# Scoring twice in the second attention of a macaron layer: by queries for the maximum, by keys for the exponential

## Chip, cores and metric

The kernel runs on one core of a Trainium2 chip. The metric is the device time in microseconds (us), the median of several executions. Three executions of the kernel before took 834.92, 836.00 and 836.39 us; the median is 836.0.

## What is computed

Two layers run one after the other on an input of 4 x 256 tokens with 256 features. Each is a macaron layer: half a feed-forward network, self-attention, half a feed-forward network, each behind a layer norm.

```python
x = x + 0.5 * ffn0(layernorm(x))          # silu(gate) * up
x = x + attn0(layernorm(x))               # 16 heads of 128, 4 key/value heads, window
x = x + 0.5 * ffn0(layernorm(x))
x = x + 0.5 * moe(layernorm(x))           # 8 experts, top 2, and a shared expert
x = x + attn1(layernorm(x))               # 16 heads of 16, causal
x = x + 0.5 * moe(layernorm(x))
```

The change lies in `attn1`, the second attention:

```python
qkv = einsum('bld,ed->ble', x, W_qkv); q, k, v = split(qkv, 3)     # to 4 x 16 heads x 256 x 16
q, k = rope(q), rope(k)
att = einsum('bhqd,bhkd->bhqk', q, k) * 16 ** -0.5
att = where(causal, att, -inf)
y = einsum('bhqk,bhkd->bhqd', softmax(att), v)
out = einsum('bld,ed->ble', y, W_o)
```

## The kernel before

The 1,024 tokens are 8 tiles of 128. A half, `hf`, is a pair of the four sequences, so 4 tiles. The kernel is one program in which every engine has its own list of instructions, written by hand; semaphores order them (`wait_ge`, `then_inc`; `after(engine, sem, n)` is a wait that is left out where it would be trivial). The six stages are told by their turn number: turn 4 is the layer norm and turning ahead of the second attention, turn 5 turns the attention's result for the output projection, turn 6 is ahead of the last feed-forward network, whose routing (`route_logits`, `prefix`, `routing_slots`, `routing_weights`, `scatter`, all with 6 and a half) is threaded through the attention's second half.

**The second attention** runs half 0 (about 581 to 630 us), then projections, rotations and turnings of half 1's queries and keys, then half 1 (about 657 to 704 us), then the output. `half(hf)` goes through 16 heads; a step, `step1(hf, p, q)`, is head g = 4p + q of the half, for both sequences of it, and every engine has its own `step1`. For each sequence the score block is causal: two query tiles of 128, the first against 128 keys, the second against 256, so 384 columns a sequence, 768 a step, in two banks of PSUM.

A head goes through these operations:

- TensorE, `scores_of`: four score matmuls with queries as weights (L1804) and four that add the mask (L1808); scores of even heads lie in banks 2hf and 2hf+1, those of odd heads in 4 and 5.
- VectorE: two maximum reductions, negated, into `MB1` (L1369).
- TensorE, the shift: four matmuls with the identity `IDB` as weights and the maximum, broadcast along the columns, as the moving operand add minus the maximum to the scores in PSUM (L1843).
- ScalarE: one exponential over the 768 columns into `PR1`, f32 (L896).
- TensorE: six f32 transposes, one for each block of 128 x 128, into banks 6 and 7 (L1821), two heads behind.
- ScalarE copies the turned probabilities as f16 (L891, `PT1[., 0]`), VectorE subtracts that from PSUM for the f16 remainder (L1375, `PT1[., 1]`).
- TensorE, the values: 18 matmuls of 17 columns (16 features and the sum of the row), three heads behind (L1504, in the helper `product`).
- VectorE: reciprocal of the sum and multiplication (L1385, L1390).

In TensorE's list, step g holds the transposes of head g-2, the values of head g-3, the shift of head g, and the scores of head g+1. `lagged(p, q, n, P1)` says whether a head n behind exists.

**Other work in the halves.** VectorE does the sums and statistics of turn 4 for half 1 (`turn_stats(4, 1, .)`) after steps 0 and 1 of half 0 and its norms (`turn_norm`, L1048) after steps 5 and 7; TensorE's `turn(4, 1)` comes near that half's end. In half 1 TensorE does `prefix(6, 0)` after step 0 (L1542, L1547) and VectorE the slots after step 0 (`routing_slots`, L1099 to L1113) and the weights after step 4 (`routing_weights`, L1138 to L1145). GpSimd's list has, for the halves, only turn 4's reciprocal roots (L522, L525) and, in half 1, `scatter(6, 0)`: eight indirect DMAs (L561) that write the tokens to the rows of their experts. Outside the halves GpSimd works in the rotations (L631, L639, L641).

`ARENA` is a region of SBUF that the stages share; the second attention keeps `PR1` (two buffers of 768 f32) and `PT1` (two buffers of two parts of 768 f16) there.

Of the kernel before, what the change touches and what calls it, by code (L numbers as in the profile page):

```python
# [88 lines left out]
def macaron(nc, x_in, wa_in, wb_in, wc_in, wd_in, wg_in, rope0_in, rope1_in, mask_in, idf_in,  # L89
# [3 lines left out]
    with ctx:  # L93
# [45 lines left out]
        ARENA = sb("ARENA", [P, 3584], F32)  # L139
# [7 lines left out]
        PT1 = ARENA[:, 1536:3072].bitcast(F16).rearrange("p (a s n) -> p a s n", a=2, s=2)  # L147
# [106 lines left out]
        exp1_done, pt1_done, pt1_hi, pt1_lo = (sem(n) for n in ("exp1_done", "pt1_done", "pt1_hi", "pt1_lo"))  # L254
# [184 lines left out]
        def pt1_part(a, s, i):  # L439

            return PT1[:, a, s, i * BLK1 * P:(i + 1) * BLK1 * P]

# [66 lines left out]
        def _(pool):  # L509
# [133 lines left out]

            turn(0, 0)
# [25 lines left out]
            turn(4, 1)  # L670
# [5 lines left out]
            scatter(6, 0)  # L676
# [7 lines left out]
        def _(act):  # L684
# [200 lines left out]
            def step1(hf, p, q):  # L885
                g = NG1 * hf + 4 * p + q
                if lagged(p, q, 2, P1):
                    after(act, pv1_done, g - 3)
                    for i in range(2):
                        act.wait_ge(pt1_done, 2 * g - 3 + i)  # L890
                        sc.activation(pt1_part(q % 2, 0, i), PS[:, 6 + i, 0:BLK1 * P], ACT.Copy).then_inc(pt1_hi, 1)  # L891
                if lagged(p, q, 0, P1):

                    act.wait_ge(shifted1, g + 1)
                    bank = 4 if q % 2 else 2 * hf
                    sc.activation(PR1[:, q % 2, :].rearrange("p (b n) -> p b n", b=2),  # L896
                                  PS[:, bank:bank + 2, 0:384], ACT.Exp, bias=LNSP[:, :],
                                  scale=SC1 / SQ ** 2).then_inc(exp1_done, 1)

            def attention1():  # L900
                def half(hf):
                    for q in range(4):
                        step1(hf, 0, q)
                    with act.Fori(1, P1) as p:
# [5 lines left out]
                    step1(hf, P1, 1)  # L910
# [62 lines left out]
        def _(dve):  # L973
# [388 lines left out]
            def step1(hf, p, q):  # L1362
                g = NG1 * hf + 4 * p + q
                a = q % 2
                if lagged(p, q, 0, P1):
                    dve.wait_ge(scores1, g + 1)
                    bank = 4 if a else 2 * hf
# [3 lines left out]
                item, turned_item = lagged(p, q, 3, P1), lagged(p, q, 2, P1)  # L1371
# [6 lines left out]
                if turned_item:  # L1378
                    low(0)
                if item:  # L1380
# [5 lines left out]
                if turned_item:  # L1386
                    low(1)
                if item:
# [4 lines left out]
            def attention1():  # L1393
                def half(hf):
# [11 lines left out]
                    with dve.Fori(2, P1) as p:  # L1406
                        for q in range(4):
                            step1(hf, p, q)
                    for q in range(3):
# [88 lines left out]
        def _(pe):  # L1498
# [299 lines left out]

            def scores_of(hf, p, q):
                bank = 4 if q % 2 else 2 * hf  # L1800
                after(pe, exp1_done, NG1 * hf + 4 * p + q - 1)
                for i in range(2):
                    for qt, c0 in ((0, 0), (1, P)):
                        te.matmul(PS[:, bank + i, c0:c0 + (qt + 1) * P],  # L1804
# [3 lines left out]
                        ins = te.matmul(PS[:, bank + i, 2 * c0:2 * c0 + P], IDB[:, :], MASK[:, :], start=False,  # L1808
                                        stop=False, skip_group_check=True)
                ins.then_inc(scores1, 1)  # L1810

            def step1(hf, p, q):
                g = NG1 * hf + 4 * p + q
                a = q % 2
                bank = 4 if a else 2 * hf
# [34 lines left out]
                elif q == 3 and lagged(p + 1, 0, 0, P1):  # L1850
                    scores_of(hf, p + 1, 0)
# [198 lines left out]
```

## Time and profile before

| | |
|---|---|
| median of three executions | 836.0 us (834.92 to 836.39) |
| span of the profiled execution | 835.5 us |
| TensorE matmul busy | 718.3 us, 86% of the span |
| TensorE weight load busy | 483.5 us, 58% |
| VectorE busy | 628.1 us, 75% |
| ScalarE busy | 458.0 us, 55% |
| GpSimd busy | 402.9 us, 48% |
| second attention, half 0 | about 581 to 630 us |
| second attention, half 1 | about 657 to 704 us |

The profiled execution has no time of its own beside its span, which lies 0.5 us under the median of the others. In the profile PE is TensorE's matmuls and PEld its weight loads (which overlap), DVE is VectorE, ACT ScalarE, POOL GpSimd, SP the engine that issues plain DMAs. PEclk is the granted TensorE clock, 1.00 for 2.4 GHz and 0.50 for 1.2 GHz. In a timeline a row is one instruction, or a run of like ones (x4), with its start in the span, its length, its engine, its line and what it writes and reads; brackets hold the idle time ahead of it and who ended it. Shares over the whole span say little about one stage; what the change is worth is read in the two halves.

### The profile page before, as it was taken

The page shows a single profiled execution, that of the slowest core. Times are in us where ns is not written, and L with a number is a line of the kernel's source. Part 1 is how long each engine was busy: PE and PEld are TensorE (multiplying, and loading weights), DVE is VectorE, ACT ScalarE, POOL GpSimd, SP SyncE. Part 2 cuts the span into 40 slices and gives each one's busy share as a digit, 9 for nine tenths or more (in the row PEclk, how much of TensorE's full clock was granted, in tenths as well). Part 3 has the DMA queues.
Part 4 walks back from the last instruction along what each step waited for, and adds up shares of the span by engine and source line. Part 5 has one row for each costly group of instructions (what it writes and reads, how often), then busy time and mean ns, then how long its engine had stood idle before and what let it go on. Part 6 is the DMA issues. An engine that isn't in the chain of part 4 may idle for free. (4 is left out here: it accounts for less than half of the span.)

```text
span 835.5 us, 17560 instructions
## 1 busy us (share of the span) xinstructions
PE 718.3 (86%) x5515; PEld 483.5 (58%) x5515; DVE 628.1 (75%) x1436; ACT 458.0 (55%) x1033; POOL 402.9 (48%) x412
## 2 busy tenths in 40 slices
PE   7898959999979999989898699855897598988985
PEld 3454437777636777755455466433785487545652
DVE  5989878778787778698987577543898596775646
ACT  3444568887757788646423266325574475324541
POOL 4545766767666676358636277424005320331440
PEclk8999989999989999999999799976799598998997
DMA  9999994000000000030001243300000010013324
GB/s 371 328 303 182 241 216 2 0 0 0 1 1 1 0 0 0 1 120 1 1 14 51 77 116 109 133 1 1 1 2 1 18 35 2 2 61 88 115 84 151
DMA packets 64945, 59.07 MB, mean 71 GB/s; under 512 B 29106, under 2 KB 59186, under 8 KB 64370
## 3 DMA queue, kind: packets, MB, share of 16 engines
q1 hardware_dynamic: 60706, 47.85, 23.5%
q0 software_dynamic: 3744, 10.26, 3.5%
q8 instruction: 36, 0.59, 0.3%
q14 instruction: 27, 0.22, 0.1%
q10 hardware_dynamic: 432, 0.15, 0.1%
HBM read 27.92 MB, written 30.33 MB: 70 GB/s over the span
## 5 line engine op out<-in xcount | busy, mean ns | idle before, releaser
L1504 PE MATMUL PS<-XT,WA 128*128 128x512 f16 x432 | 101.2, 382 | 0.0
L611 POOL TENSOR_TENSOR ARENA<-ARENA,ST 128x512 f32<-128x512 f32 x64 | 66.6, 1040 | 65.5 <-DVE ST L1284 65.5
L729 ACT ACTIVATE ARENA<-T 128x512 f16<-128x512 f32 (+1 forms) x56 | 35.2, 628 | 109.2 <-DVE T L1162 101.7
L1504 PE MATMUL PS<-WA,ARENA 128*128 128x256 f16 (+2 forms) x960 | 68.4, 213 | 12.7 <-DVE ARENA L1171 11.7
L1504 PEld LDWEIGHTS PS<-WA,ARENA 128*128 128x128 f16 x960 | 56.6, 97 | 29.0 <-DVE ARENA L1171 17.6
L570 POOL DMA_INDIRECT yt_rows<-WA,DIX x46 | 45.4, 987 | 55.0 <-ACT WA L861 41.0
L1504 PEld LDWEIGHTS PS<-XT,WA 128*128 128x128 f16 (+1 forms) x432 | 42.6, 99 | 44.9 <-issue 2.1
L1264 DVE TENSOR_REDUCE ST<-PS 128x2 f32<-128x512 f32 x64 | 44.0, 687 | 27.7 <-PE PS L1504 26.7
L1504 PE MATMUL PS<-KVR,ARENA 128*128 (+1 forms) x384 | 58.2, 280 | 7.5 <-DVE ARENA L1256 4.6
L1504 PE MATMUL PS<-XT,WC 128*128 128x512 f16 x264 | 62.3, 387 | 2.4 <-DVE T L1155 1.4
L762 ACT ACTIVATE ARENA<-PS,ST 128x256 f32<-128x256 f32 x128 | 59.3, 470 | 7.0 <-DVE ST L1267 6.8
L599 POOL TENSOR_TENSOR T<-T 128x512 f32<-128x512 f32 x40 | 52.6, 1315 | 8.1 <-DVE T L1250 2.6
L594 POOL TENSOR_TENSOR T<-T,ROPE 128x512 f32<-128x512 f32 x40 | 50.9, 1271 | 10.4 <-ACT T L743 10.3
L1171 DVE TENSOR_TENSOR ARENA<-T,ARENA 128x512 f16<-128x512 f32 (+1 forms) x48 | 43.0, 896 | 16.1 <-ACT ARENA L729 15.6
L1504 PE MATMUL PS<-ARENA,KVR 128*128 128x256 f16 x384 | 52.4, 272 | 2.5 <-DVE ARENA L1287 2.5
L1504 PE MATMUL PS<-XT,WB 128*128 128x512 f16 x192 | 48.5, 391 | 6.2 <-DVE T L1250 4.8
L1504 PE MATMUL PS<-WB,ARENA 128*128 (+1 forms) x384 | 52.4, 273 | 0.3 <-DVE ARENA L1287 0.3
L1155 DVE SCALAR_TENSOR_TENSOR T<-T,PS 128x512 f32<-128x512 f32 (+1 forms) x56 | 38.1, 680 | 18.8 <-ACT T L721 18.4
L721 ACT ACTIVATE T<-PS 128x512 f32<-128x512 f32 (+1 forms) x56 | 33.1, 592 | 33.9 <-PE PS L1504 33.7
L1504 PE MATMUL PS<-WE,WA 128*128 x276 | 50.1, 318 | 0.0
L1504 PE MATMUL PS<-WC,ARENA 128*128 128x256 f16 (+1 forms) x288 | 41.0, 299 | 8.9 <-DVE ARENA L1171 8.8
L1504 PEld LDWEIGHTS PS<-KVR,ARENA 128*128 128x128 f16 x384 | 33.0, 100 | 26.5 <-issue 7.4
(184 smaller groups left out, 1799.5 us busy)
## 6 DMA issues: line engine op xcount, KB each, us to landing
xs_rows<-ROUT SPq DMA_DIRECT2D x2, 9252.0 KB, 45.9
WA<-xs_rows SPq DMA_DIRECT2D x46, 129.0 KB
WB<-wb_dram SPq DMA_DIRECT2D x1, 4096.0 KB, 21.6
WC<-wc_dram SPq DMA_DIRECT2D x1, 2304.0 KB, 27.3
WA<-wa_dram SPq DMA_DIRECT2D x4, 512.0 KB, 7.3
WA<-wa_dram SPq DMA_DIRECT2D x1, 2048.0 KB, 12.9
WA<-yt_rows SPq DMA_DIRECT2D x4, 512.0 KB, 4.1
WB<-yt_rows SPq DMA_DIRECT2D x4, 512.0 KB, 6.0
```

Of the source, the lines that this page charges most:

```text
L570: pl.indirect_dma_start(YT, bass.IndirectOffsetOnAxis(ap=DIX[:, b:b + 1], axis=0), YB[:, g % 3, :], None, bounds_check=2 * ROWS + 2 * TOK ...
L594: pl.tensor_tensor(t2, t2, ROPE0[:, 1:2, :].broadcast_to([P, 2, S]), ALU.mult).then_inc(rope_sin, 1)
L599: pl.tensor_tensor(T1[:, a, :], T1[:, a, :], T2[:, a, :], ALU.add).then_inc(rope_sum, 1)
L611: pl.tensor_tensor(pr, pr, rs.broadcast_to([P, 2, S]), ALU.mult).then_inc(norm_done, 1)
L721: sc.activation(T1[r, 0, :], PS[r, GATE[a], :], ACT.Tanh, scale=0.5 / (SX * SW)).then_inc(tanh_done, 1)
L729: sc.activation(HH[r, a, 0, :], T3[r, :], ACT.Copy).then_inc(hid_hi, 1)
L762: sc.activation(PR0[:, x % 2, qt * S:(qt + 1) * S], PS[:, bank, qt * S:(qt + 1) * S], ACT.Exp, bias=ST[:, x % 2, 1, qt:qt + 1], scale=SC0 ...
L1155: v.scalar_tensor_tensor(T2[r, 0, :], T1[r, 0, :], 1.0, PS[r, GATE[a], :], ALU.add, ALU.mult).then_inc(gated, 1)
L1171: v.tensor_tensor(HH[r, a, 1, :], T3[r, :], HH[r, a, 0, :], ALU.subtract).then_inc(hid_lo, 1)
L1264: v.tensor_reduce(ST[:, x % 2, 0, :], PS[:, bank, :].rearrange("p (q k) -> p q k", q=2), AX.X, ALU.max).then_inc(max_done, 1)
L1504: ins = te.matmul(dst, left(a), right(b), start=first and n == 0, stop=last and n == 2, skip_group_check=True)
```

## The change

Scores are formed twice. `scores_of`, by queries, now serves the maximum alone and always writes banks 2hf and 2hf+1, with one mask matmul for a sequence in place of two (the two diagonal blocks in one instruction, 2 x 128 columns). A new `turned_scores` forms the same scores with keys as weights, so that they stand turned in PSUM, in banks 4 and 5 or 6 and 7, with their own masks. The shift adds the maximum to the turned scores: since queries now run along the columns, the broadcast maximum is the weights and `IDB` moves. ScalarE does the exponential of the turned scores twice, once as f16 (`PT1[q, 0]`) and once as f32 (`PR1`), and GpSimd subtracts the one from the other (L647 of the new file, `PT1[q, 1]`). The six transposes, ScalarE's two copies and VectorE's two subtractions are gone, with the semaphore `pt1_done`. The values follow two heads behind, not three. `PT1` has four buffers, and `ARENA` is larger by 1,024 f32 a partition.

GpSimd's list gets `half1`: a subtraction for each step, turn 4's roots behind subtractions 0 and 1 of half 0, and in half 1 `scatter(6, 0)` in parts: the DMAs of tiles 0, 1 and 2 behind subtractions 3, 5 and 7, those of tile 3 behind the last. On TensorE `turn(4, 1)` moves ahead of the last two value groups, and values(15) ahead of the next half's first projection.

```diff
+            def step1(hf, p, q):
+                g = NG1 * hf + 4 * p + q
+                pool.wait_ge(exp1_done, g + 1)
+                pl.tensor_tensor(PT1[:, q, 1, :], PR1[:, q % 2, :], PT1[:, q, 0, :], ALU.subtract).then_inc(pt1_lo, 1)
+
+            def half1(hf):
+                for p in range(2):
+                    for q in range(4):
+                        step1(hf, p, q)
+                        if (hf, p) == (0, 0) and q < 2:
+                            turn(4, 1, (q,))
+                        if hf and p * 4 + q in (3, 5, 7):
+                            scatter(6, 0, ((p * 4 + q) // 2 - 1,))
+                with pool.Fori(2, P1) as p:
+                    for q in range(4):
+                        step1(hf, p, q)
...
-            turn(4, 1)
+            half1(0)
...
-            scatter(6, 0)
+            half1(1)
+            scatter(6, 0, (3,))
             run_glu(pool, 3, 0, glu_step, glu_side)
...
             def step1(hf, p, q):
                 g = NG1 * hf + 4 * p + q
-                if lagged(p, q, 2, P1):
-                    after(act, pv1_done, g - 3)
-                    for i in range(2):
-                        act.wait_ge(pt1_done, 2 * g - 3 + i)
-                        sc.activation(pt1_part(q % 2, 0, i), PS[:, 6 + i, 0:BLK1 * P], ACT.Copy).then_inc(pt1_hi, 1)
...
+                act.wait_ge(shifted1, g + 1)
+                bank = exp_bank(q % 2)
+                after(act, pv1_done, g - 3)
+                sc.activation(PT1[:, q, 0, :].rearrange("p (b n) -> p b n", b=2), PS[:, bank:bank + 2, 0:384], ACT.Exp,
+                              bias=LNSP[:, :], scale=SC1 / SQ ** 2).then_inc(pt1_hi, 1)
+                after(act, pt1_lo, g - 1)
+                sc.activation(PR1[:, q % 2, :].rearrange("p (b n) -> p b n", b=2), PS[:, bank:bank + 2, 0:384], ACT.Exp,
+                              bias=LNSP[:, :], scale=SC1 / SQ ** 2).then_inc(exp1_done, 1)
...
-                def low(i):
-                    dve.wait_ge(pt1_hi, 2 * g - 3 + i)
-                    v.tensor_tensor(pt1_part(a, 1, i), PS[:, 6 + i, 0:BLK1 * P], pt1_part(a, 0, i),
-                                    ALU.subtract).then_inc(pt1_lo, 1)
...
             def scores_of(hf, p, q):
...
-                        ins = te.matmul(PS[:, bank + i, 2 * c0:2 * c0 + P], IDB[:, :], MASK[:, :], start=False,
-                                        stop=False, skip_group_check=True)
+                    ins = te.matmul(diagonal(bank), IDB[:, :], twice(MASK[:, :]), start=False, stop=True,
+                                    skip_group_check=True)
                 ins.then_inc(scores1, 1)
+
+            def turned_scores(hf, p, q):
+
+                after(pe, exp1_done, NG1 * hf + 4 * p + q - 1)
+                for i in range(2):
+                    bank = exp_bank(q % 2) + i
+                    for kt in range(2):
+                        te.matmul(PS[:, bank, 2 * kt * P:2 * P + kt * P],
+                                  KZ1[:, 4 * p + q, i * S + kt * P:i * S + (kt + 1) * P],
+                                  QT1[:, 2 * p + q // 2, i * S + kt * P:(i + 1) * S], start=kt == 0, stop=False,
+                                  skip_group_check=True)
+                    te.matmul(diagonal(bank), MASK[:, :], twice(IDB[:, :]), start=False, stop=False,
+                              skip_group_check=True)
...
-                if lagged(p, q, 2, P1):
-                    pe.wait_ge(exp1_done, g - 1)
                     for i in range(2):
-                        after(pe, pt1_lo, 2 * g - 5 + i)
-                        for j in range(BLK1):
-                            ins = te.transpose(PS[:, 6 + i, j * P:(j + 1) * P],
-                                               PR1[:, a, (BLK1 * i + j) * P:(BLK1 * i + j + 1) * P], IDF[:, :])
-                        ins.then_inc(pt1_done, 1)
...
+                        bank = exp_bank(a) + i
+                        for qt in range(2):
+                            shift = MB1[:, a, 2 * qt + i:2 * qt + i + 1].broadcast_to([P, P])
+                            ins = te.matmul(PS[:, bank, qt * P:(1 + 2 * qt) * P], shift,
+                                            twice(IDB[:, :]) if qt else IDB[:, :], start=False, stop=qt == 1,
+                                            skip_group_check=True)
+                    ins.then_inc(shifted1, 1)
+                ahead = (p, q + 1) if q < 3 else (p + 1, 0)
+                more = lagged(ahead[0], ahead[1], 0, P1)
+                if more:
+                    scores_of(hf, *ahead)
+                if item := lagged(p, q, 2, P1):
...
+                    pe.wait_ge(pt1_lo, g - 1)
+                    after(pe, o1_done, g - 3)
...
+                if more:
+                    turned_scores(hf, *ahead)
...
-                    step1(hf, P1, 0)
                     if hf == 0:
                         turn(4, 1)
+                    step1(hf, P1, 0)
                     step1(hf, P1, 1)
...
                 queries_keys1(1, 0, TPH)
-                step1(0, P1, 2)
```

A step in the list of TensorE (PS is the PSUM, MB the maxima, IDB and IDF identities, KVR keys and queries, WA the values' weights region, ARENA the probabilities). Before:

```order
L1821 MATMUL PS<-IDF,ARENA 128x128 [waits pt1_lo,exp1_done]
L1821 MATMUL PS<-IDF,ARENA 128x128 x2
L1821 MATMUL PS<-IDF,ARENA 128x128 [waits pt1_lo]
L1821 MATMUL PS<-IDF,ARENA 128x128 x2
L1504 MATMUL PS<-WA,ARENA 128x17 [waits pt1_lo]
L1504 MATMUL PS<-WA,ARENA 128x17 x17
L1843 MATMUL PS<-MB,IDB 128x128 [waits shift1_done]
L1843 MATMUL PS<-MB,IDB 128x256
L1843 MATMUL PS<-MB,IDB 128x128
```

The same place in the changed list:

```order
L1846 MATMUL PS<-IDB,MB 128x256
L1815 MATMUL PS<-KVR 128x128
L1815 MATMUL PS<-KVR 128x256
L1819 MATMUL PS<-MASK,IDB 128x2x128
L1815 MATMUL PS<-KVR 128x128
L1815 MATMUL PS<-KVR 128x256
L1819 MATMUL PS<-MASK,IDB 128x2x128
L1508 MATMUL PS<-WA,ARENA 128x17 [waits pt1_lo]
L1508 MATMUL PS<-WA,ARENA 128x17 x17
L1829 MATMUL PS<-KVR 128x256 [waits exp1_done]
L1829 MATMUL PS<-KVR 128x128
L1833 MATMUL PS<-IDB,MASK 128x2x128
```

The transposes ahead of the values are gone; the scores by keys (L1829, with their mask L1833) stand behind the values and wait for the exponentials that last read their banks.

GpSimd's list, second half (XN holds the normed tokens, IDX their rows). Before, the last rotation, then the scatters in one piece, then the next stage:

```order
L641 TENSOR_TENSOR ARENA<-T,ARENA 128x16x32
L561 DMA xs_rows<-XN,IDX 9216x258 [waits idx_done,dma_z]
L561 DMA xs_rows<-XN,IDX 9216x258 x7
L545 TENSOR_TENSOR ARENA<-T,ARENA 128x512 [waits hid_hi]
```

In the changed list:

```order
L641 TENSOR_TENSOR ARENA<-T,ARENA 128x16x32
L647 TENSOR_TENSOR ARENA<-ARENA 128x768 [waits exp1_done] x4
L561 DMA xs_rows<-XN,IDX 9216x258 [waits idx_done,dma_z]
L561 DMA xs_rows<-XN,IDX 9216x258
L647 TENSOR_TENSOR ARENA<-ARENA 128x768 [waits exp1_done] x2
L561 DMA xs_rows<-XN,IDX 9216x258 [waits idx_done,dma_z]
L561 DMA xs_rows<-XN,IDX 9216x258
L647 TENSOR_TENSOR ARENA<-ARENA 128x768 [waits exp1_done] x2
```

The subtractions now stand ahead of the scatters and between them.

TensorE's list at the second half's first step, around the prefix (MSK is the routing mask). Before:

```order
L1808 MATMUL PS<-MASK,IDB 128x128
L1542 MATMUL PS<-MSK,LOW 128x32 [waits sel_done]
L1547 MATMUL PS<-MSK,ONES 128x32
L1547 MATMUL PS<-MSK,ONES 128x24
L1547 MATMUL PS<-MSK,ONES 128x16
```

In the changed list:

```order
L1819 MATMUL PS<-MASK,IDB 128x2x128
L1829 MATMUL PS<-KVR 128x256 [waits exp1_done]
L1829 MATMUL PS<-KVR 128x128
L1833 MATMUL PS<-IDB,MASK 128x2x128
L1829 MATMUL PS<-KVR 128x256
L1829 MATMUL PS<-KVR 128x128
L1833 MATMUL PS<-IDB,MASK 128x2x128
L1546 MATMUL PS<-MSK,LOW 128x32 [waits sel_done]
```

Head 1's scores by keys have come between its scores by queries and the prefix.

## Rows read from the trace of the kernel before

**Rows 1.** Busy us by stretch (xinstructions): PE, PEld, DVE, ACT, POOL, PEclk, DMA, GB/s.

```profile
600.00:622.00 22.00, 21.19 (x352) 19.31 (x349) 21.69 (x62) 16.62 (x30) 0.00 (x0) 1.00 0.01 2
657.30:668.00 10.70, 7.20 (x50) 5.82 (x51) 4.93 (x14) 2.87 (x5) 3.12 (x4) 0.50 0.08 26
```

**Rows 2.** Timeline, one step, all engines: start us, us, engine line operation [idle before].

```profile
610.22 0.28 PEld L1843 LDWEIGHTS PS<-MB,IDB 128*128 128x128 bf16 x4
...
610.77 0.90 ACT L896 ACTIVATE ARENA<-PS,LNSP 128x768 f32<-128x768 f32 x1 [0.42 <-PE PS L1843]
...
611.07 0.22 PE L1808 MATMUL PS<-MASK,IDB 128*128 128x128 bf16 x1
...
611.12 0.82 PE L1821 MATMUL PS<-IDF,ARENA 128*128 128x128 f32 x6
611.32 1.02 DVE L1369 TENSOR_REDUCE MB<-PS 128x2 bf16<-128x256 f32 x2
...
611.78 0.68 PE L1504 MATMUL PS<-WA,ARENA 128*128 x18
612.26 0.55 DVE L1375 TENSOR_TENSOR ARENA<-PS,ARENA 128x384 f16<-128x384 f32 x1
612.40 0.28 PEld L1843 LDWEIGHTS PS<-MB,IDB 128*128 128x128 bf16 x4
```

**Rows 3.** Timeline, GpSimd alone, at three places.

```profile
486.74 0.43 POOL L536 TENSOR_TENSOR WB<-WB 128x128 f16<-128x128 f32 x1
...
665.35 0.97 POOL L561 DMA_INDIRECT xs_rows<-XN,IDX  x1 [0.30 <-issue]
...
714.88 1.15 POOL L545 TENSOR_TENSOR ARENA<-T,ARENA 128x512 f16<-128x512 f32 x1 [40.89 <-ACT ARENA L729]
```

**Rows 4.** Timeline, GpSimd and VectorE, where both work.

```profile
643.32 1.27 POOL L631 TENSOR_TENSOR T<-T 128x512 f32<-128x512 f32 x1
643.39 1.67 DVE L1048 TENSOR_SCALAR XN<-X,MV,RSTD 128x256 f32<-128x256 f32 x2 [0.31 <-POOL RSTD L525]
...
715.72 0.66 DVE L1017 SCALAR_TENSOR_TENSOR X<-PS,X 128x512 f32<-128x512 f32 x1
```

**Rows 5.** Timeline, VectorE, the norms in the first half.

```profile
599.35 1.02 DVE L1369 TENSOR_REDUCE MB<-PS 128x2 bf16<-128x256 f32 x2
...
601.41 0.73 DVE L1048 TENSOR_SCALAR XN<-X,MV,RSTD 128x256 f32<-128x256 f32 x2
602.06 1.02 DVE L1369 TENSOR_REDUCE MB<-PS 128x2 bf16<-128x256 f32 x2
```

**Rows 6.** Timeline, all engines, the second half's first steps.

```profile
660.54 0.90 ACT L896 ACTIVATE ARENA<-PS,LNSP 128x768 f32<-128x768 f32 x1 [3.28 <-PE PS L1843]
...
661.94 0.22 DVE L1106 TENSOR_TENSOR ROUT<-ROUT 128x64 f32<-128x64 f32 x1
...
662.98 1.02 DVE L1369 TENSOR_REDUCE MB<-PS 128x2 bf16<-128x256 f32 x2
```

**Rows 7.** Timeline, VectorE, maxima 4, the weights' first operation, maxima 5 and 11.

```profile
670.95 1.02 DVE L1369 TENSOR_REDUCE MB<-PS 128x2 bf16<-128x256 f32 x2
...
673.02 0.24 DVE L1138 TENSOR_TENSOR ROUT<-ROUT 128x64 f32<-128x64 f32 x1
...
674.37 1.02 DVE L1369 TENSOR_REDUCE MB<-PS 128x2 bf16<-128x256 f32 x2
...
688.12 1.02 DVE L1369 TENSOR_REDUCE MB<-PS 128x2 bf16<-128x256 f32 x2
```

**Rows 8.** Timeline, VectorE, the ends of both halves.

```profile
622.34 1.02 DVE L1369 TENSOR_REDUCE MB<-PS 128x2 bf16<-128x256 f32 x2
...
630.23 0.68 DVE L1340 TENSOR_TENSOR T<-PS,ROPE 128x512 f32<-128x512 f32 x1
...
696.93 1.02 DVE L1369 TENSOR_REDUCE MB<-PS 128x2 bf16<-128x256 f32 x2
...
703.55 0.18 DVE L1385 RECIPROCAL R<-PS 128x4 f32<-128x4 f32 x1 [0.61 <-PE PS L1504]
```

More of the change, by code:

```diff
@@ L146, in macaron @@
         PR1 = ARENA[:, 0:1536].rearrange("p (a n) -> p a n", a=2)
-        PT1 = ARENA[:, 1536:3072].bitcast(F16).rearrange("p (a s n) -> p a s n", a=2, s=2)
+        PT1 = ARENA[:, 1536:4608].bitcast(F16).rearrange("p (a s n) -> p a s n", a=4, s=2)
         ROUT = sb("ROUT", [P, 1536], F32)
@@ L437, in v_bank, with exp_bank @@
             return 2 * hf + i % 2
-        def pt1_part(a, s, i):
-            return PT1[:, a, s, i * BLK1 * P:(i + 1) * BLK1 * P]
+        def exp_bank(a):
+            return 4 + 2 * a
         def up_bank(f, a):
@@ L903, in half @@
                         step1(hf, 0, q)
-                    with act.Fori(1, P1) as p:
+                    with act.Fori(1, P1 - 1) as p:
                         for q in range(4):
                             step1(hf, p, q)
-                    step1(hf, P1, 0)
+                    for q in range(4):
+                        step1(hf, P1 - 1, q)
                     if hf == 0:
                         turn_high(4, 1)
-                    step1(hf, P1, 1)
                     turn_high(5, hf)
@@ L1366, in step1 @@
                     dve.wait_ge(scores1, g + 1)
-                    bank = 4 if a else 2 * hf
+                    bank = 2 * hf
                     for qt, cols in ((0, slice(0, P)), (1, slice(P, 3 * P))):
@@ L1405, in half @@
                                 routing_weights(6, 0)
-                    with dve.Fori(2, P1) as p:
+                    with dve.Fori(2, P1 - 1) as p:
                         for q in range(4):
                             step1(hf, p, q)
+                    for q in range(4):
+                        step1(hf, P1 - 1, q)
                     for q in range(3):
@@ L1797, in turn_qk, with diagonal, twice @@
                 ins.then_inc(qk1_turned, 1)
+            def diagonal(bank):
+                return PS[:, bank, 0:BLK1 * P].rearrange("p (b n) -> p b n", b=BLK1)[:, 0:BLK1:2, :]
+            def twice(x):
+                return x.rearrange("p (o n) -> p o n", o=1).broadcast_to([P, 2, P])
             def scores_of(hf, p, q):
-                bank = 4 if q % 2 else 2 * hf
-                after(pe, exp1_done, NG1 * hf + 4 * p + q - 1)
                 for i in range(2):
+                    bank = 2 * hf + i
                     for qt, c0 in ((0, 0), (1, P)):
-                        te.matmul(PS[:, bank + i, c0:c0 + (qt + 1) * P],
+                        te.matmul(PS[:, bank, c0:c0 + (qt + 1) * P],
                                   QT1[:, 2 * p + q // 2, i * S + qt * P:i * S + (qt + 1) * P],
@@ L1833, in step1 @@
                                 ins = product(PS[:, odd_bank(hf) + b, c0:c0 + VC1],
[L1834 removed]
+                                              lambda s: PT1[:, item[1], s, blk * P:(blk + 1) * P],
                                               lambda s: VB1[:, s, TPH * hf + 2 * i + kt, h, :], kt == 0, kt == qt)
                     ins.then_inc(pv1_done, 1)
[L1837 to L1851 removed]
+                if more:
+                    turned_scores(hf, *ahead)
             def attention1():
```

40 lines of the change are left out of this document (7 added, 33 removed).

## The prediction

> **What bounds the kernel now.** I read the busy time by stretch first, to find the second attention and its TensorE clock; then the timeline of all engines through one step of it at full clock; then the timeline of each place where something else is done between the steps; last, GpSimd's rows wherever it does work like the work it is now given. A step is one head of one pair of sequences. There are 16 in each half of the stage, and I call them step 0 to 15.
>
> Between 600 and 622 us TensorE was busy for 21.19 of 22 us, VectorE for 21.69 and ScalarE for 16.62, at the full clock; the second half opens at half clock [rows 1]. At full clock a step takes 2.18 us: the load that opens the shift stands at 610.22 and again at 612.40 [rows 2]. The reader should see a ring in these rows. Shift of head g and scores of head g+1 run from 610.22 to the end of the last mask matmul, 611.07 + 0.22 = 611.29; the two maxima start 0.03 later and last 1.02, to 612.34; 0.06 later the next shift starts. 1.07 + 0.03 + 1.02 + 0.06 = 2.18, the whole step, with no other engine in it. TensorE's own list is nearly as long: shift and scores 0.90 (to 611.12), transposes 0.66 (to 611.78), values 0.62 (to 612.40), together 2.18. VectorE's is too: two maxima, two subtractions of 0.55, the division. ScalarE has a pass of 0.90 and two copies. Three things end together, and only the ring remains if the other two get shorter.
>
> **The change part by part.** I write s for the start of a step's shift.
>
> *The steady step: nothing.* The ring is kept: shift, scores by queries, maxima, with as many columns as before in fewer instructions. The shift's weights now hold the maximum, but the load of the shift stood behind the maximum before, too (610.22). I count no gain and no loss. Removed from TensorE: six f32 transposes, 0.66. Added: scores by keys with their masks, the same 1,280 columns as the scores by queries. Shift and scores are 2,048 columns in 0.90, 0.44 ns each, so 0.56. 0.90 + 0.62 + 0.56 = 2.08, under the ring by 0.10. This cover is thin: a tenth lost beyond it, in forms of matmul that no row shows, would cost 2 to 3 us over the stage. ScalarE: two passes of 0.90, 1.80, hidden under 2.18. VectorE loses both subtractions and keeps the maxima and the division. The larger ARENA, the fourfold PT1 and the dropped semaphore cost nothing.
>
> *GpSimd's subtraction, 768 wide.* No row shows this width. The same form took 0.43 at 128 columns and 1.15 at 512 [rows 3]: on that line 768 is 1.15 + 0.72 x 256/384 = 1.63; in plain proportion 1.73. I take 1.65, nearest to the line, and keep both. Inside a step it is hidden. The f32 pass ends at s + 0.55 + 1.80 = 2.35 (610.22 to 610.77 is the 0.55), GpSimd runs from s + 2.40 to 4.05, and values are wanted at s + 2 x 2.18 + 0.90 = 5.26.
>
> The Trainium skill (GPSIMD Engine Reference, 4.1 Engine selection) says that elementwise work with two inputs belongs on VectorE, GpSimd being about twice as slow. By that rule the step would no longer hide it, and the sum would be rival D's, 848.1.
>
> *VectorE held up by GpSimd.* This decides most. At 643.39 two normalising operations of L1048, which take 0.73 [rows 5], took 1.67, and ended only after GpSimd's 643.32 + 1.27 = 644.59 [rows 4]. An operation that reads PSUM, 715.72, which started while GpSimd's 714.88 ran [rows 3], took 0.66 for its 512 columns [rows 4], as another took 0.68 at 630.23 [rows 8]. So VectorE's work from SBUF to SBUF waits for a running GpSimd operation, and the maxima, which read PSUM, don't. Until now GpSimd was idle in the halves but for short work; now it is busy for 1.65 of every 2.18, from s + 0.22 to s + 1.87 of the next step's time.
> - First half, norms of turn 4, after two steps. Before: 599.35 to 602.06 is 2.71, so 0.53 each [rows 5]. Now they could start at about s + 0.30, are held to 1.87, and end at 2.60; the next maxima were due at s + 1.10. 1.50 each. 2 x (1.50 - 0.53) = **+1.9**.
> - Second half, slots. Step 0's exponentials start at 660.54 [rows 6]; 1.80 later, at 662.34, and 0.05 for the signal, GpSimd starts; it ends at 664.04. L1106, the second operation of the slots, would start at 663.04 (661.94, and 1.1 by the next term). **+1.0**.
>
> *Second half, the prefix.* VectorE's slots wait for the prefix on TensorE, and only then does VectorE take maxima(1) (662.98) [rows 6]. Scores by keys of head 1 now stand ahead of the prefix: 1,280 columns, at half clock 2 x 0.56: **+1.1**. Scores(0) by keys hide behind the maxima(0).
>
> *The low clock.* Maxima 1 to 4 took 662.98 to 670.95 [rows 6, 7], 7.97 for three steps, 1.43 over three of 2.18. TensorE's unbroken work begins 2.1 later now. A low-clock step by TensorE's list is 2 x (0.90 + 0.56) + 0.62 = 3.5. I take **+0.3**, with bounds of -1.4 (the clock is up when they begin) and +2 (one or two more such steps).
>
> *Second half, scatters between the subtractions.* Eight scatters ran on an idle GpSimd, each 0.97 with 0.30 ahead [rows 3]; now two stand behind subtraction 3, 5 and 7, 2.45 a pair. From s of step 4: subtraction 3 ends at 1.87. The weights, held until then, last 1.35 (673.02 to 674.37), so maxima(5) start at 3.22 and s of step 5 is 4.30. Scatters to 4.32; subtraction 4 to 5.97; head 5's second pass ends at 4.30 + 2.35, so subtraction 5 runs from 6.70 to 8.35; scatters to 10.80; 6 and 7 to 14.10; scatters to 16.55; 8 to 18.20. Values(6), due at 4.30 + 3 x 2.18 + 0.90 = 11.74, wait for 12.45 and put off the rest by 0.7; values(8), due at 16.8 then, wait for 18.20, and step 11's shift follows 1.3 later, at 19.5. Before, maxima 4 to 11 took 670.95 to 688.12, 17.17, with the weights among them [rows 7]. **+2.4**. Behind it GpSimd catches up by 0.5 a step. The last pair of scatters comes after subtraction 15; the loads that need them also wait for the scatters of tokens 6, 1, which are issued much later.
>
> *The two ends.* First half: from the end of maxima(15), 623.36, to the first rotation on VectorE, 630.23, are 6.87 [rows 8]. Now: 0.06 + 0.55 to the first pass, 1.80, 0.05, 1.65, 0.06, values 0.68, then the projection's six matmuls of 512 columns, 1.35, now behind the values: 6.2. **-0.6**. Second half: 697.95 to the last division, 703.55, is 5.60; now 0.61 + 1.80 + 0.05 + 1.65 + 0.06 + 0.68 + 0.06 = 4.91. **-0.7**. Turn(4, 1), moved ahead of values(14) on TensorE, fills a wait there.
>
> Sum: first half +1.3, second half 1.0 + 1.1 + 0.3 + 2.4 - 0.7 = +4.1; together **+5.4**. Behind the stage everything waits for it, so all of it arrives. The profiled execution has a span of 835.5; the three timed runs have a median of 836.0, 0.5 above it, which I take for what lies around the span. The forecast is 836.0 + 5.4 = 841.4.
>
> **The rivals.**
> A. *VectorE isn't held up*, or goes first. For: in the first half the norms could start at s + 0.30 and GpSimd's subtraction at 0.22, nearly together. Against: [rows 4]. The norms then hide in VectorE's free time, -1.1 where it was +1.9; slots 0 for 1.0; the weights cost 0.6 of their 1.35, and the line of subtractions and scatters +1.6 for 2.4. -1.1 - 0.6 + 1.1 + 0.3 + 1.6 - 0.7 = +0.6: 836.6, no change that can be told. The Trainium skill (SBUF — State Buffer, Who interferes with whom) says that whichever of the two starts first keeps the shared port for its whole instruction; by that, a norm that starts first would pass unhindered.
> B. *Faster: the subtraction is so short that the scatters fit.* Its place is GpSimd's line in the second half. Two subtractions and a pair of scatters must fit in two steps: (4.36 - 2.45) / 2 = 0.95 is where it decides. Then, with A, the line slips nowhere, the weights give back 0.7, and both ends shorten by another 0.7: -1.1 - 0.6 - 0.7 + 1.1 + 0.3 - 0.7 - 1.4 = -3.1, 832.9. Against: 512 columns took 1.15.
> C. *The clock is up sooner*, since scores by keys add columns where TensorE stood idle at half clock: it was busy for 7.20 of 10.70 [rows 1]. Both halves then lose their low-clock steps, 2 x 1.43, and half of the prefix term, 0.5: 841.4 - 3.4 = 838.0. Against: those columns come in the gaps between steps, which stay.
> D. *The subtraction takes 2.2*, twice VectorE's two of 0.55 [rows 2], and no longer fits a step. Norms 2 x 0.55; 11 steps of the first half at 2.26, +0.9; both ends 2 x 0.55; slots 0.55; GpSimd's line to step 11 at 22.3, +2.8, and the steps behind it +0.3: +6.7, 848.1. Against: [rows 3], by which it takes 1.65.
>
> **How the numbers follow.** Forecast 0.64, its own range 838.5 to 845.5 (the low-clock bounds, 1.63 and 1.73, and TensorE's list over the ring by 0.1); A 0.12, B 0.07, C 0.09, D 0.08. The range 836.5 to 845.5 takes in A and C and leaves out B, D and a twentieth of the forecast above. A difference of 0.2%, 1.7 us, is about what can be told from none. Faster: B and a little, 0.08. Same: A and what of C falls short, 0.14. Slower: 0.78.
>
> **What would show it.** The steady step in the new profile: still 2.15 to 2.2 between maxima, each starting 0.04 after the last mask matmul; if TensorE's list has become the bound, the maxima start at once but the shift waits for the scores by keys. GpSimd's rows of 768: 1.6 to 1.75. The two norms: a pair of some 2.3 instead of 0.73. Slots and prefix: maxima(1) about 2.1 later after step 0. In the second half TensorE should wait for GpSimd ahead of values(6) and (8). If the norms and L1138 keep their old times, the hold is wrong and A is right; if no wait stands ahead of values(8), the line of scatters is; if the granted clock of either half's start differs by more than one step, that term is.

## The result, and the profile after

The changed kernel took 838.59 us (median of six, 838.32 to 840.31), the kernel before beside it 835.83 (834.40 to 837.23). The ratio is 1.0045, 95% interval 1.0024 to 1.0067: slower by 0.45%, 3.8 us. The forecast was 841.4, from 836.5 to 845.5. The sign and the range held; of the 5.4 us, some two thirds came by the ratio, half by the medians, which are 2.8 apart.

The page's first part, of the changed kernel:

```profile
span 838.5 us, 17314 instructions
...
PE 718.0 (86%) x5451; PEld 475.9 (57%) x5451; DVE 606.4 (72%) x1372; ACT 455.3 (54%) x1001; POOL 455.1 (54%) x444
```

VectorE has lost 22 us and GpSimd gained 52, its 32 subtractions; TensorE's busy time is what it was. So the time went into waits. Where, I read from VectorE's timelines, as the forecast did: the starts of the first maxima, of the first rotation, of the last division.

| stretch (us) | before | after | difference | forecast |
|---|---|---|---|---|
| up to the first maxima of the first half | 582.30 | 582.90 | +0.6 | 0 |
| first half, to the first rotation behind it | 47.93 | 49.79 | +1.9 | +1.3 |
| between the halves | 28.37 | 28.96 | +0.6 | 0 |
| second half, to its last division's start | 44.95 | 49.17 | +4.2 | +4.1 |
| behind the stage | 131.95 | 127.68 | -4.3 | 0 |

The stage cost what was forecast, and more; then 4.3 us came back behind it, in code that the change doesn't touch. Both need an account.

**The hold.** The timeline of GpSimd and VectorE in the changed kernel, at the second pair of norms, where [rows 5] had 0.73:

```profile
605.69 1.64 POOL L647 TENSOR_TENSOR ARENA<-ARENA 128x768 f16<-128x768 f32 x1 [1.00 <-ACT ARENA L911]
605.76 2.04 DVE L1062 TENSOR_SCALAR XN<-X,MV,RSTD 128x256 f32<-128x256 f32 x2
...
607.72 1.01 DVE L1383 TENSOR_REDUCE MB<-PS 128x2 bf16<-128x256 f32 x2
```

The subtraction takes 1.64, as estimated. The norms start 0.07 behind it and last 2.04; the maxima, which read PSUM, last 1.01 beside any subtraction. In the second half the slots and the weights, where [rows 6, 7] had single operations of about 0.2:

```profile
664.99 0.19 DVE L1113 TENSOR_TENSOR ROUT<-PS,K 128x32 f32<-128x32 f32 x1 [2.31 <-PE PS L1551]
...
665.36 1.64 POOL L647 TENSOR_TENSOR ARENA<-ARENA 128x768 f16<-128x768 f32 x1 [9.16 <-ACT ARENA L911]
...
665.73 1.32 DVE L1123 TENSOR_TENSOR ROUT<-ROUT,KB 128x32 f32<-128x32 f32 x1
...
676.85 1.64 POOL L647 TENSOR_TENSOR ARENA<-ARENA 128x768 f16<-128x768 f32 x1 [1.12 <-ACT ARENA L911]
...
676.92 1.65 DVE L1152 TENSOR_TENSOR ROUT<-ROUT 128x64 f32<-128x64 f32 x1
...
680.83 0.80 PE L1846 MATMUL PS<-IDB,MB 128*128 128x128 bf16 x4 [1.22 <-DVE MB L1383]
```

Each held operation ends with the subtraction (665.36 + 1.64 = 667.00, against 667.05; 678.49 against 678.57). The last row is what follows the weights: TensorE waits 1.22 for maxima(5), and then works at half clock.

**The values.** Here the forecast saw nothing. Timeline of the changed kernel, all engines, steps 8 to 13 of the first half; [rows 2] is the like step before:

```profile
609.86 1.12 PE L1508 MATMUL PS<-WA,ARENA 128*128 x18
609.94 1.02 DVE L1383 TENSOR_REDUCE MB<-PS 128x2 bf16<-128x256 f32 x2 [0.86 <-PE PS L1819]
...
611.48 0.49 PE L1846 MATMUL PS<-IDB,MB 128*128 128x128 bf16 x4
...
612.39 1.11 PE L1508 MATMUL PS<-WA,ARENA 128*128 x18
612.58 1.02 DVE L1383 TENSOR_REDUCE MB<-PS 128x2 bf16<-128x256 f32 x2 [1.13 <-PE PS L1819]
...
619.75 0.60 PE L1508 MATMUL PS<-WA,ARENA 128*128 128x17 f16 x18
```

The 18 value matmuls take 1.1 in six of the loop's eight steps (4 to 11), 0.67 to 0.74 in the other two, and 0.60 behind it. The shift (611.48) starts 0.5 after the maxima are done. Maxima come 2.64 and 2.52 apart there, and VectorE's idle time ahead of them (0.86, 1.13) ends with TensorE's mask.

### The profile page after: what moved, and what is told of

Read it like the earlier page. It is cut to its first block and busy times, and to the rows that moved or that the text cites. A ratio compares the mean times of both kernels' runs of the same rounds, so it can differ in the third digit from the quotient of the medians.

```text
span 838.5 us, 17314 instructions
## 1 busy us (share of the span) xinstructions
PE 718.0 (86%) x5451; PEld 475.9 (57%) x5451; DVE 606.4 (72%) x1372; ACT 455.3 (54%) x1001; POOL 455.1 (54%) x444
## 5 line engine op out<-in xcount | busy, mean ns | idle before, releaser
L1508 PE MATMUL PS<-WA,ARENA 128*128 128x256 f16 (+2 forms) x960 | 74.0, 215 | 15.9 <-DVE ARENA L1185 11.7
L1508 PEld LDWEIGHTS PS<-WA,ARENA 128*128 128x128 f16 x960 | 59.2, 98 | 36.6 <-DVE ARENA L1185 17.6
L647 POOL TENSOR_TENSOR ARENA<-ARENA 128x768 f16<-128x768 f32 x32 | 52.4, 1641 | 43.8 <-ACT ARENA L911 43.8
L570 POOL DMA_INDIRECT yt_rows<-WA,DIX x46 | 45.2, 982 | 53.2 <-ACT WA L879 41.8
L1383 DVE TENSOR_REDUCE MB<-PS 128x2 bf16<-128x256 f32 x64 | 32.6, 551 | 32.7 <-PE PS L1819 32.7
L908 ACT ACTIVATE ARENA<-PS,LNSP 128x768 f16<-128x768 f32 x32 | 28.8, 900 | 40.0 <-PE PS L1846 40.0
```

The lines of the kernel that those rows point to most:

```text
L570: pl.indirect_dma_start(YT, bass.IndirectOffsetOnAxis(ap=DIX[:, b:b + 1], axis=0), YB[:, g % 3, :], None, bounds_check=2 * ROWS + 2 * TOK ...
L647: pl.tensor_tensor(PT1[:, q, 1, :], PR1[:, q % 2, :], PT1[:, q, 0, :], ALU.subtract).then_inc(pt1_lo, 1)
L1508: ins = te.matmul(dst, left(a), right(b), start=first and n == 0, stop=last and n == 2, skip_group_check=True)
```

## The experiments

Each edit is against the changed kernel unless it says otherwise. The expectations count what lies behind the stage to the end of VectorE's last operation; the tables here count it to the span's end, 2.6 later in the changed kernel.

**Loop written out.**

```diff
-                    with pe.Fori(1, P1 - 1) as p:
+                    for p in range(1, P1 - 1):
                         for q in range(4):
                             step1(hf, p, q)
```

> The changed kernel with TensorE's loop over heads 4 to 11 written out, so that its operands have fixed addresses. In the changed kernel the 18 value matmuls take 1.1 us in the loop's steps and 0.60 behind it, with gaps of 0.1 us among them. Then the values take 0.60 to 0.68 everywhere, steps 8 to 13 of the first half go from 12.2 us (607.72 to 619.95) to 10.9, and the second half (first maxima to last division, 49.2) loses about 1.0, since GpSimd's line of subtractions and scatters holds part of it. Rival: the gaps come from the operands (GpSimd writing the same region while TensorE reads it); then the values still take 1.1 and both halves stay within 0.3.

The values take 0.60 to 0.68 everywhere; steps 8 to 13 of the first half lasted 10.8 us, the second half 47.6, 1.5 less. The first half as a whole lost only 0.3 (49.5), because maxima 3 to 4 took 3.25 for 2.23, at a clock that rose three microseconds later. The values themselves decide: the theory holds and the rival falls. One line's statistics between 604 and 622 us, first of the changed kernel, then of this one (instructions, then least, median and longest ns):

```profile
L1508 PE MATMUL PS<-WA,ARENA x130: 170/171/183, 604.3 to 622.0; 128*128 x108, 128*128 128x17 f16 x22
L1508 PEldq FUSED_REGOPS  x46: 46/46/79, 604.1 to 617.9; - x46
```

```profile
L1508 PE MATMUL PS<-WA,ARENA x144: 170/171/174, 605.3 to 622.0; 128*128 128x17 f16 x144
```

```profile
L1504 PEldq FUSED_REGOPS  x40: 46/46/79, 604.1 to 614.3; - x40
```

Either kernel has 64 of them for the values in each half, eight a step. Before, in the step of [rows 2], five of the eight run beside the six transposes and three among the values. In the changed kernel's first half, one runs ahead of the values and seven among them wherever the values take 1.1; four or five run ahead where they take 0.67 to 0.74. The total, 839.68 (ratio 1.0061, 1.0032 to 1.0090), did not follow: behind the stage this run took 132.0.

**Scatters last.**

```diff
-                        if hf and p * 4 + q in (3, 5, 7):
-                            scatter(6, 0, ((p * 4 + q) // 2 - 1,))
...
-            scatter(6, 0, (3,))
+            scatter(6, 0)
```

> The changed kernel with all eight scatters of tokens 6, 0 behind the last subtraction of the second half. Theory: in steps 5 to 10 TensorE's values wait for GpSimd's line; without the scatters maxima 5 to 11 of the second half go from 16.0 us (679.75 to 695.73) to about 14.6, where TensorE's loop still costs some 0.3 in most steps; the scatters end some 8 us later than now, and nothing waits for them. Rival: these steps are long through TensorE's loop alone; then 16.0 stays. Second rival: the loads of the routed tokens wait for the scatters, and what the half gains comes back behind the stage.

Maxima 5 to 11 took 16.9 us, not 14.6 (the changed kernel has 16.0): the theory falls here. In the changed kernel, between 680 and 700 us, TensorE waits for GpSimd nowhere; the table of its waits there has two rows:

```profile
PE PS L1846 <- DVE MB L1383: 1.2, 1, 1.2
PE PS L1846 <- issue: 0.2, 1, 0.2
```

Without the scatters, subtraction 4 starts at 677.8 rather than 681.0 and holds a second operation of the weights (1.49 for 0.17): maxima 4 to 5 took 5.36 for 4.12. TensorE's clock was then 0.50 from 680.7 to 686.0, over two steps of 3.01 and 3.25. Behind the stage this run took 131.6, like others at the same clock, so the second rival isn't seen. 845.75 in all (1.0145, 1.0104 to 1.0185), the slowest of the versions; of the 7.2 between its median and the changed kernel's, 2.6 lie in the second half of the two traces, and why all four executions were that slow stays open.

**Norms and weights moved.**

```diff
-                            if hf == 0 and p and q in (1, 3):
-                                turn_norm(4, 1, (q // 2,))
+                            if (hf, p, q) == (0, 0, 2):
+                                turn_norm(4, 1)
...
-                            if hf and (p, q) == (1, 0):
-                                routing_weights(6, 0)
...
+                        if (hf, q) == (1, 0):
+                            routing_weights(6, 0)
```

> The changed kernel with the norms of turn 4 moved to VectorE's idle time behind step 2 of the first half, where GpSimd is idle for 2 us, and the routing weights moved behind the last maxima of the second half. Theory: both were held by GpSimd's subtraction (norm pairs 1.98 and 2.04 for 0.73, the weights' first operation 1.65 for 0.24). Then the norm pairs take 0.73 again, steps 5 to 8 of the first half go from 8.7 us to 6.6 (1.1 below the kernel before's 7.6 is the time of the norms themselves), and in the second half maxima 4 to 5 go from 4.12 to 2.18; the half-clock stretch at 681 us, which follows that wait, goes too, and step 5 with it from 2.98 to 2.2. First half -2.1, second half -2.7. Rival: VectorE's operations are longer for another reason (their place in the list, the larger region); then the norms still take 2 and the halves gain less than 1.

The norm pairs took 0.73 and 0.74, and maxima 4 to 5 of the second half 2.17: the hold is shown. But steps 5 to 8 took 7.5, not 6.6, since the loop's gaps now showed there (2.66, 2.63), and the slots, still beside GpSimd, took as long as in the changed kernel's second execution below (maxima 0 to 1, 6.24). First half 48.5 (-1.3), second 47.8 (-1.3), about half of what was expected; 842.02 in all (1.0093, 1.0052 to 1.0133), with 132.7 behind the stage.

**Prefix first.** The prefix moves from behind step 0 into it, between scores by queries and by keys.

> The changed kernel with the prefix matmuls of the second half ahead of head 1's scores by keys. Theory: the slots then run before GpSimd's first subtraction (which starts at 665.36), the operation that took 1.32 takes 0.19, and maxima 0 to 1 of the second half go from 5.73 us to 4.4. Rival: the slots were late through the exponentials or the clock; then maxima 0 to 1 stay above 5.3.

Maxima 0 to 1 took 5.28, between the two. The operation that was held is free, but the next-but-one is caught:

```profile
665.21 0.19 DVE L1123 TENSOR_TENSOR ROUT<-ROUT,KB 128x32 f32<-128x32 f32 x1
665.33 1.64 POOL L647 TENSOR_TENSOR ARENA<-ARENA 128x768 f16<-128x768 f32 x1 [9.27 <-ACT ARENA L911]
665.43 0.19 DVE L1126 TENSOR_REDUCE XN<-ROUT 128x4 f32<-128x32 f32 x1
665.65 1.34 DVE L1127 CAST IDX<-ROUT 128x8 int32<-128x8 f32 x1
```

The slots came 0.3 us too late to be clear of the subtraction. The reduction among them was not held. The second half took 47.3, 1.9 less, of which this step has 0.4; two others ran at full clock here (maxima 2 to 3 in 2.17 for 3.01, 5 to 6 in 2.17 for 2.98). 841.15 (1.0081, 1.0043 to 1.0118).

**All of them.** The four edits, and a wait for GpSimd:

```diff
                 pool.wait_ge(exp1_done, g + 1)
+                if isinstance(p, int) and (hf, p, q) == (1, 0, 0):
+                    pool.wait_ge(idx_done, 3)
```

> The changed kernel with the four edits together (loop written out, scatters last, norms and weights moved, prefix first), and GpSimd's first subtraction of the second half waiting for the slots. Theory: nothing is held up any more. First half (first maxima to first rotation) 46.5 us where the kernel before has 47.9 and the changed one 49.8; second half (first maxima to last division) 42.5 where they have 45.0 and 49.2. What lies behind the stage takes 125 to 130 us, by how many half-clock stretches fall into it, so 829 to 834 in all, below the kernel before run beside it. Rival: the scores by keys have made the ring itself slower or GpSimd's subtraction holds up the maxima too; then the halves stay above the kernel before's.

829.73 us (829.01 to 831.68), ratio to the kernel before 0.9942 (0.9922 to 0.9963): the only version shown to beat it, by 0.58%. The halves took 45.6 and 40.6. From step 4 on every step of either half is 2.17, the ring that the forecast read in [rows 2]. Its timeline, two steps of the first half:

```profile
603.28 0.60 PE L1508 MATMUL PS<-WA,ARENA 128*128 128x17 f16 x18
603.49 1.02 DVE L1383 TENSOR_REDUCE MB<-PS 128x2 bf16<-128x256 f32 x2 [0.80 <-PE PS L1819]
604.56 0.28 PEld L1846 LDWEIGHTS PS<-IDB,MB 128*128 128x128 bf16 x4 [0.34 <-DVE MB L1383]
605.46 0.60 PE L1508 MATMUL PS<-WA,ARENA 128*128 128x17 f16 x18
605.65 1.02 DVE L1383 TENSOR_REDUCE MB<-PS 128x2 bf16<-128x256 f32 x2 [0.80 <-PE PS L1819]
```

TensorE now waits for VectorE (0.34) and VectorE for TensorE (0.80), which is what a ring without a full engine looks like.

**The changed kernel again.**

> The changed kernel once more, unchanged, beside the same runs of the kernel before as the others. Theory: the two halves take 49.8 and 49.2 us again, since what they lose is fixed by the order of the work; what lies behind them takes 125 us again or up to 130, with the half-clock stretches, so 836 to 842 in all. Rival: the recovery of 4 us behind the stage is a property of the change; then it is 125 again in every run, and 838.5 in all.

839.15 (1.0055, 1.0037 to 1.0073). The profiled execution had halves of 49.4 and 48.3 and 132.4 behind the stage, where the first had 127.7. So the 4.3 us don't come back in every execution. This one was the slowest of the eleven (844.93), and the 6 to 7 us that the stage costs in the two profiles are more than the 4.5 between the medians: how much comes back in a usual execution isn't known. The second half differs as well: maxima 0 to 1 took 6.24, since the operation held among the slots was L1120 (1.38 for 0.23), and the step behind the weights 2.31 for 2.98, at a clock that stayed at 1.00.

**The loop of the kernel before written out.** The same edit as the first, in the kernel before.

> The kernel before with the same loop of TensorE written out. Theory: there the gaps among the values lie under the ring or the transposes, and only the 0.1 to 0.55 by which a few steps of the second half exceed 2.18 goes: first half within 0.3 of 47.9, second half within 0.8 of 45.0. Rival: writing the loop out gains about 1.5 us in each half in any version of the kernel, so that the gaps have nothing to do with the change.

First half 47.4 (-0.5), second 44.0 (-0.95), both a little outside what was expected, and 834.25 in all, ratio 0.9992 (0.9972 to 1.0011): no difference. The first half's 0.5 is not the loop's: the next run, with the loop in place there, has 47.4 too. In the kernel before, then, the address operations cost nothing in the first half and under 1 us in the second.

**The kernel before, made late.** Twelve reductions ahead of the second half's last division.

> The kernel before with twelve reductions of no use on VectorE, about 7 us, ahead of the last division of the second half, so that its end comes as late as in the changed kernel. Theory: what follows the stage isn't shortened by being late; it takes 125 to 130 us as its half-clock stretches fall, and each microsecond less of half clock there goes with some 0.4 less of time. Rival: something that runs beside the stage (a transfer) bounds what follows, so that lateness of 7 us is partly absorbed; then it takes 125 with the half-clock stretches unchanged.

The second half took 51.1, 6.1 more, and what follows 128.9 at a mean granted clock of 0.92. The run before it, with the same code behind the stage, the same clock and no delay, took 129.8 there: of the 6.1, at most 0.9 was absorbed, by one trace of each (838.54 here, one execution).

**Taken back one by one.** The last three start from the version with all five edits and undo one part: the scatters, the loop, the norms with the weights. The prefix and GpSimd's wait were not taken back.

> The version with all five edits, but with the scatters of tokens 6, 0 between the subtractions again, as in the changed kernel. This prices the scatters alone. Theory: GpSimd then has three pairs of 2.45 us more in nine steps with 0.53 to spare in each; the 40.6 us of the second half become 41.5 to 43, in one or two steps at whose values TensorE waits for GpSimd. Rival: since the subtraction waits two steps anyway, the line absorbs the scatters; 40.6 stays.

> The version with all five edits, but with TensorE's loop back. This prices the loop alone. Theory: the eight steps of the loop take 2.2 to 3.0 instead of 2.17, some 2.5 us in each half: 45.6 becomes 48 in the first half and 40.6 becomes 43 in the second. Rival: the gaps show only where another wait has made TensorE late; then each half gains less than 1.

> The version with all five edits, but with the norms and the weights where they were. This prices what VectorE loses beside GpSimd. Theory: the norm pairs take 2 us again and the steps with them 3.3, so 45.6 becomes 47.9 in the first half, less 0.4 to 0.7 if VectorE's idle time behind step 2 isn't used; in the second half the weights' step takes 4.1 to 5.4 for 2.17 and may bring a half-clock stretch: 40.6 becomes 42.6 to 45. Rival: with TensorE's loop written out there is room for them; then both halves stay within 1.

| version (us) | first half | second half | one execution |
|---|---|---|---|
| all five | 45.6 | 40.6 | 829.7 (median) |
| scatters back | 45.2 | 44.9 (+4.3) | 833.06 |
| loop back | 48.8 (+3.3) | 44.1 (+3.6) | 836.32 |
| norms and weights back | 46.2 (+0.7) | 45.4 (+4.9) | 831.21 |

With the loop back its steps are 2.19 to 3.12, the pattern of the changed kernel, with no other wait about. With the scatters back, and the loop out of the way, TensorE does wait for GpSimd ahead of the values, as forecast, and three times (values 4, 6 and 8):

```profile
672.57 0.61 PE L1510 MATMUL PS<-WA,ARENA 128*128 128x17 f16 x18 [0.65 <-POOL ARENA L649]
...
678.27 0.61 PE L1510 MATMUL PS<-WA,ARENA 128*128 128x17 f16 x18 [1.48 <-POOL ARENA L649]
...
683.98 0.62 PE L1510 MATMUL PS<-WA,ARENA 128*128 128x17 f16 x18 [1.49 <-POOL ARENA L649]
```

A half-clock stretch of 3.5 us follows the last. With norms and weights back, the norms' steps took 3.34 and 3.26 and the weights' step 5.36, with two steps of 3.00 and 3.25 at half clock behind it. The first half's 2.3 for the norms is partly made up for by steps 2 to 4, which were 1.2 shorter there: without the norms among them, and at full clock from 590 on, where the version with all five fell to 0.50 between 592 and 594.

**What lies behind the stage.** Windows from the last division to the span's end, in the first execution of the changed kernel and in the second (us, then busy us of PE, PEld, DVE, ACT and POOL, the granted clock, the DMA share, GB/s):

```profile
710.82:838.50 127.68, 107.10 (x721) 67.02 (x721) 84.09 (x226) 49.21 (x124) 38.41 (x41) 0.93 0.26 84
```

```profile
710.67:843.10 132.43, 111.00 (x721) 68.59 (x721) 84.03 (x226) 49.34 (x124) 38.46 (x41) 0.90 0.25 81
```

The same 721 matmuls, from the same time on; VectorE and ScalarE are as busy, TensorE 3.9 longer. Over all thirteen traces the length of this window goes with its mean granted clock: at 0.90 it is 131.4 to 132.7 (before, loop written out, scatters last, norms moved, changed again, scatters back), at 0.92 it is 128.9 to 130.9 (four), at 0.93 127.7 to 129.5 (three). When the stage ended doesn't decide it: at 0.90 the window starts between 699.7 and 711.6. Nor does the change, since the changed kernel has both 0.93 and 0.90. Whether another version favours one level isn't shown, with one trace of each; and that the clock is the cause, and not what goes with it, is argued from the matmuls' busy time alone.

## Why the prediction was right, and where it was wrong

The sums come near the measured stretches partly by luck. The second half's +4.2 for +4.1 is made of a prefix that cost 0.9 less than the forecast, slots 0.1 more, the steps with the scatters 0.5 more and for another reason, the ends 0.2 less, and 0.5 for maxima 11 to 15, where the forecast had nothing. By its total alone, 838.59, the run lies nearer to rival C's 838.0 than to the forecast.

- *The steady step: nothing.* Wrong, and the largest miss in mechanism. Maxima 8 to 15 of the first half took 16.57 for 15.40, +1.2; priced alone the loop costs 3.3 and 3.6. The step that failed is TensorE's list, 0.90 + 0.62 + 0.56 = 2.08: the 0.62 for values was read where six transposes of 0.66 stood ahead, under which the sequencer worked out most of the addresses. The change took that cover away, and the values became 1.1. The sign named for it came: the maxima that start at 609.94 end at 610.96, but the next shift starts at 611.48, behind the scores by keys. With fixed addresses the list holds, and steps are 2.17. The forecast called the cover thin and looked for its loss in the new forms of matmul; it was lost in the old ones.
- *GpSimd's subtraction.* Right: 1.64 for 1.65. Rival D falls. The factor of about two (the Trainium skill, GPSIMD Engine Reference, 4.1 Engine selection) doesn't come out beside VectorE's two of 0.55, of which 1.64 is 1.5 times; but those read PSUM, and no run here has this subtraction on VectorE from SBUF.
- *VectorE held up.* Right in mechanism, which the moves and their undoing show; rival A falls. The Trainium skill (SBUF — State Buffer, Who interferes with whom) has whoever starts first keep the port; the traces agree for the held operations, all of which started behind a subtraction. The other case isn't among them. The norms were mis-sized: the steps with them took 3.32 and 3.25 for 2.71, +1.1 for +1.9, since the first of the pair ends with the subtraction and only the second, 0.41, comes behind it, where I had put both. The slots, +1.1 for +1.0, by L1123, and in the second execution by L1120, the operation that the forecast named.
- *The prefix.* +0.22 (3.34 from maxima(0) to the slots, for 3.12) where I had +1.1. The clock rose at 663.7, just ahead of those columns, and fell again at 667: rival C in small, worth 0.9. In the second execution it rose at 665.5, behind most of them, and the prefix cost 0.70. *The low clock:* in the second half maxima 1 to 4 took 8.25 for 7.97, +0.3 as forecast; in the first it rose sooner, and maxima 3 to 4 came 2.23 apart for 3.19, a gain of 1.0 that the sum had at nothing. That gain is an execution's: the same two maxima are 3.17 apart in the second one, and 2.68 in the kernel before made late.
- *Scatters and weights.* Maxima 4 to 11 took 20.10 for 17.17, +2.9 for +2.4: the sum near, the reason in part wrong. The weights' hold is there (4.12 for 3.42), but the wait ahead of values(6) and (8) is not: the steps had become so long, through the loop's gaps and the half clock, that GpSimd kept up. What took its place is the loop, and 0.8 in one step at half clock behind the weights (0.50 from 680.9 to 684.3). Of two things that stretch the same steps only the longer shows; with the loop away, the scatters cost their 4.3.
- *The ends.* Second half 5.76 for 6.62, -0.9 for -0.7: right. First half 8.40 for 7.89, +0.5 for -0.6: TensorE waited 1.55 for the last subtraction, and the projection behind it ran at half clock (0.50 between 629.7 and 633.1), which the sum had at full clock. With the scatters last, where the first half's code is the same, the clock was 1.00 there and the end took 7.14, -0.7 as the sum had it (its terms give 0.67, not the 0.6 that it was entered with). *Between the halves* the forecast had nothing; it was +0.6, and +1.3 in the second execution, and no run says why.
- *"Behind the stage everything waits for it, so all of it arrives."* Wrong in that execution by 4.3 and right in the next, 132.4: the step took what follows as fixed, and it moves by 4 to 5 us with the clock. That is nearly as large as the whole forecast. The 0.5 that the forecast put around the span is 1.8 in this execution (840.31 for 838.5); the sum, which goes from median to median, doesn't use it.

## What to carry to other kernels

Before you take work off an engine's list, ask what it covered: here the transposes hid the address operations of a loop, and a list that was 0.10 under its bound on paper was 0.4 over it in most steps. Work given to an idle GpSimd held up the norms, the cast and the two-input operations of VectorE from SBUF to SBUF that started beside it, however small (0.17 became 1.34 to 1.49); a reduction (0.19) was not held. Such operations are moved to where GpSimd waits, or GpSimd is made to wait for them. Judge a stage by its own stretch in several traces, since what lies behind it can move by more than the stage gained.

## What was not expected

- Single edits, each meant to take out one wait (ratios 1.0061 to 1.0145), left the kernel slower than before, and one left it 7 us slower than the changed kernel; all of them together made it 0.58% faster than before. In the halves the waits lay over one another.
- The same 721 matmuls behind the stage took 127.7 to 132.7 us, at a mean granted clock of 0.93 to 0.90. What sets the half-clock stretches in one execution and not in another stays open; no run here fixed them.
